# Grouped-query attention in two layers on one core: every scaling of the probabilities on GpSimd as a product of two tensors, and VectorE's copy of turned probabilities ahead of a row maximum

## The chip, the core and the metric

The kernel runs on one core of a Trainium2 chip. The core has engines that each work through their own list of instructions in order: TensorE (PE, with its weight loads PEld), VectorE (DVE), ScalarE (ACT), GpSimd (POOL) and SyncE (SP, which here only starts transfers). They meet at semaphores alone: an instruction that waits holds up everything behind it on its engine. The metric is the device time of one execution in microseconds (us), as a median of several executions. The clock of TensorE has two levels, 1.2 and 2.4 GHz; a profile shows the share that was granted (1.00 is 2.4 GHz).

## The reference, cut to what matters

The program is two transformer layers on 16 sequences of 512 tokens with 256 features. The change lies in the first layer's attention, which has 16 query heads and 4 key/value heads of width 64:

```
scores = einsum('bhqd,bhkd->bhqk', Q, K_rep) / scale
scores = scores + polarity_bias + (1.0 - gtp) * NEG
attn = softmax(scores, axis=-1)
out = einsum('bhqk,bhkd->bhqd', attn, V_rep)
```

The mask in it is causal, so a tile of 128 queries needs only the keys up to its own end. The layer goes on with a projection, a second attention with 16 heads of width 16, and a mixture of experts; the second layer has an attention and a feed-forward part of its own.

## The kernel before, in words

The first layer works on one sequence after another. The time of one sequence is a frame of 128 beats, numbered r = 0 to 127 in the code; each engine's list is written by a loop over the beats, and for each beat a chain of `if r ...` lines says which functions are called, in which order. That hand-written order is the only thing that decides what stands behind what. Beats 0 to 63 belong to the narrow attention, beats 64 to 127 to the grouped-query attention; small matrix products of other parts ("fills") are strewn between.

The grouped-query half takes 32 pairs p = 4g + qt: g = 0 to 7 is a pair of query heads, qt = 0 to 3 the tile of 128 queries, and i = 0 or 1 the head in the pair. I call the four pairs of one g a group, i = 0 the even and i = 1 the odd part. A part with qt has (qt + 1) * 128 key columns: 128, 256, 384 or 512. A part goes through these stations:

- TensorE, `scores_g` (L699): both parts of two neighbouring pairs (qt 0 and 1, or qt 2 and 3) at once, every fourth beat.
- VectorE, `biased_max` (L974): adds the bias, writes the sum to `prob` and takes the negative row maximum.
- ScalarE, `exponentials_g` (L1248): the exponential in place, and the row sums.
- VectorE, `reciprocal_g` (L980): the reciprocals of both sums of a pair.
- GpSimd, `scale` (L1420): multiplies the part by the reciprocal. In the odd parts of qt 0 and 1 VectorE does this, inside `reciprocal_g` (L984).
- TensorE, `turn_g` (L710): turns the 128x128 tiles into PSUM bank 4 (even) or 5 (odd); a part waits until that bank was copied out for the pair before.
- The copy of the turned part to SBUF: on VectorE for the even part (`copy_g`, L993), on ScalarE for the odd one (`copy_g`, L1258).
- TensorE, `values_g` (L727): the products with V, after every second pair.

The stations of a pair lie some beats apart. At the beats r = 64 + 2p and the next, TensorE issues the scores of pairs p and p + 1 (p even) and then turns pair p - 3; VectorE takes the maxima of pair p, the reciprocal of pair p - 1 and the copy of pair p - 3. ScalarE's list is written so:

```
if r >= 65:
    exponentials_g(f, (r - 65) // 2, (r - 65) % 2)
if r >= 72 and r % 2 == 0:
    copy_g(f, (r - 72) // 2)
```

so that it does the even and the odd exponential of pair p, and behind the odd one the copy of the odd part of pair p - 3. No fill of TensorE stands between the turning of qt = 3 and that of the next qt = 0 in four of the seven groups of a frame that reach it; where qt 1 and 2 are turned, there nearly always is one.

Of the kernel before, what the change touches and what calls it, by code (L numbers as in the profile page):

```python
# [23 lines left out]
P = 128  # L24
# [425 lines left out]
def layer0(nc, a, x1_d, xf_d, gt_d, bias_d, K):  # L450

    ctx = ExitStack()
    with ctx:
# [81 lines left out]
        def bias_of(h):  # L535
# [8 lines left out]
            sem(n) for n in ("scores_ready", "max_ready", "split", "max_turned", "max_placed", "t_ready", "exp_ready", "pv_ready", "out_turned"))  # L544
        s.g_scores, s.g_max, s.g_exp, s.g_recip, s.g_scaled, s.g_scaled_v, s.g_turned, s.g_copied_v, s.g_copied_a, s.g_pv, s.g_out = (
            sem("g_" + n) for n in ("scores", "max", "exp", "recip", "scaled", "scaled_v", "turned", "copied_v", "copied_a", "pv", "out"))
        s.w_ready = sem("w_ready")
# [14 lines left out]
        def at(u):  # L562
            return u // UNITS, u % UNITS // (NT * H), u // H % NT, u % H

        def scaled_on_pool(p, i):
            return i == 0 or p % NT > 1

        def scaled(b, p, i):
            qt = p % NT
            if scaled_on_pool(p, i):  # L570
                return s.g_scaled, 6 * (PAIRS * b + p // NT) + (1, 2, 3, 5)[qt] + i
            return s.g_scaled_v, 2 * (PAIRS * b + p // NT) + qt + 1

# [63 lines left out]
        with nc.Block() as block:  # L637
            @block.tensor
            def _(pe):
# [62 lines left out]
                def turn_g(b, p, i):  # L702
                    qt = p % NT
                    v = UNITS * b + 2 * p + i
                    if p == 0:
                        pe.wait_ge(s.exp_ready, UNITS * (b + 1))
                    pe.wait_ge(*scaled(b, p, i))
                    wait(pe, (s.g_copied_v, s.g_copied_a)[i], BEATS * b + p)
# [229 lines left out]
            def _(dve):  # L938
# [38 lines left out]
                def reciprocal_g(b, p):  # L977
                    k = 2 * p
                    dve.wait_ge(s.g_exp, UNITS * b + 2 * p + 2)
                    nc.vector.reciprocal(recip_g[:, k:k + 2], sums_g[:, k:k + 2]).then_inc(s.g_recip, 1)  # L980
                    if not scaled_on_pool(p, 1):
                        dve.wait_ge(s.g_recip, BEATS * b + p + 1)
                        v = prob[p % NT][:, 1, :]
                        nc.vector.tensor_scalar(v, v, recip_g[:, k + 1:k + 2], None, ALU.mult).then_inc(s.g_scaled_v, 1)  # L984

# [144 lines left out]
                for n in range(FIRST, LAST):  # L1130
                    f, r = n // FRAME, n % FRAME
                    c = f + 1
                    if there(f):
                        if r < 64:
                            row_max(UNITS * f + r)
                        if r >= 64:
                            biased_max(f, (r - 64) // 2, r % 2)
                        if r >= 67 and r % 2:
                            reciprocal_g(f, (r - 67) // 2)
                        if r >= 71 and r % 2:  # L1140
                            copy_g(f, (r - 71) // 2)
                    if there(f - 1):
                        if r == 1:
                            reciprocal_g(f - 1, 31)
                        if r in (1, 3, 5):
                            copy_g(f - 1, 29 + (r - 1) // 2)
                        if r == 28:
# [251 lines left out]
            def _(pool):  # L1399
# [16 lines left out]
                def scale(b, p, i):  # L1416
                    qt = p % NT
                    k = 2 * p + i
                    pool.wait_ge(s.g_recip, BEATS * b + p + 1)
                    nc.gpsimd.tensor_scalar(prob[qt][:, i, :], prob[qt][:, i, :], recip_g[:, k:k + 1], None, ALU.mult).then_inc(s.g_scaled, 1)  # L1420

# [39 lines left out]
                for n in range(FIRST, LAST):  # L1461
# [6 lines left out]
                    if there(f):  # L1468
                        if r < 64 and r % 4 == 3:
                            split(QUADS * f + r // 4)  # L1470
                        if r >= 68:
                            if scaled_on_pool((r - 68) // 2, r % 2):
                                scale(f, (r - 68) // 2, r % 2)
                        if r in (6, 8, 12, 13, 17, 18):
# [906 lines left out]
```

## Time and profile before

| | |
|---|---|
| median of 3 runs | 4328.75 us (4321.15 to 4343.08) |
| the profiled execution | 4331.27 us |
| its span, first to last instruction | 4329.4 us |
| mean granted clock | 0.974 |
| busy: TensorE / VectorE / ScalarE / GpSimd | 90% / 69% / 60% / 56% of the span |

The span has the first layer's sixteen frames (to about 2780 us; the copies of `Wo`, one at each frame's end, are started at 259.57, 429.71, 600.98 us and so on, some 168 us apart), then the experts and the second layer. A row of the timeline gives start, duration, engine, line, operation, tiles, and in brackets how long the engine had been idle before it and for whom. Starts and durations are those of one execution; durations of matmuls are partly modelled, so a step that ends on TensorE is best read from start to start.

### The profile page before, as it was taken

To read this page: it belongs to the slowest core of one execution; us is meant where nothing else is said; L and a number is where in the kernel's file an instruction comes from. 1 tells how busy PE (TensorE), PEld (TensorE's weight loads), DVE (VectorE), ACT (ScalarE), POOL (GpSimd) and SP (SyncE) were. 2 spreads that over 40 slices of the span, in tenths; PEclk is the share of its full clock that TensorE was granted. 3 is DMA by queue.
4 is the path that set the end of the run, shared out by engine and by line. 5 is a ranking of instruction groups with operands and counts; after the bars stand their busy time and mean duration, and the time that the engine had idled before them with its cause. 6 is when DMAs were issued, how large, how long until landed. Compare 5 with 4: busy or idle time off the path is not lost. (4 is left out here: it accounts for less than half of the span.)

```text
span 4329.4 us, 105712 instructions
## 1 busy us (share of the span) xinstructions
PE 3895.7 (90%) x37596; PEld 2560.4 (59%) x37596; DVE 3007.5 (69%) x8821; ACT 2581.9 (60%) x6209; POOL 2412.5 (56%) x3854
## 2 busy tenths in 40 slices
PE   3999999999999999999999999739599999999998
PEld 1565656556656556656565566526366666666666
DVE  4676776776777767767767676561577778778786
ACT  2656556556566566565565565402377777777776
POOL 3656557566576575565665664525455545555552
PEclk7999999999999999999999999959799999999999
DMA  4323334334243243343342432223422424334231
GB/s 128 72 77 86 80 76 94 74 89 94 59 104 79 70 91 77 75 89 79 84 94 66 97 83 66 69 75 61 66 53 48 69 46 59 61 48 68 46 56 26
DMA packets 168566, 317.06 MB, mean 73 GB/s; under 512 B 21680, under 2 KB 112112, under 8 KB 162928
## 3 DMA queue, kind: packets, MB, share of 16 engines
q1 hardware_dynamic: 162928, 300.88, 32.6%
q0 software_dynamic: 3968, 5.25, 0.7%
q8 instruction: 305, 5.00, 0.5%
q10 hardware_dynamic: 1152, 4.19, 0.3%
q14 instruction: 213, 1.74, 0.2%
HBM read 126.66 MB, written 32.59 MB: 37 GB/s over the span
## 5 line engine op out<-in xcount | busy, mean ns | idle before, releaser
L1420 POOL TENSOR_SCALAR l_prob_wo<-l_prob_wo,l_recip_g 128x384 f32<-128x384 f32 (+3 forms) x768 | 926.8, 1217 | 265.5 <-DVE l_recip_g L980 261.5
L1871 DVE TENSOR_REDUCE l_neg_max<-l_bank 128x1 f32<-128x512 f32 x1024 | 680.2, 684 | 260.6 <-PE l_bank L1710 258.9
L1997 ACT ACTIVATE l_pts<-l_bank 128x512 f32<-128x512 f32 x1024 | 593.0, 596 | 297.3 <-PE l_bank L1725 288.4
L1248 ACT ACTIVATE l_prob_wo<-l_prob_wo,l_neg_max_g 128x128 f32<-128x128 f32 (+3 forms) x1024 | 571.2, 559 | 299.1 <-DVE l_neg_max_g L974 293.2
L961 DVE CUSTOM_DVE_ANT_0 l_bank<-l_bank,l_mask 128x128 f32<-128x128 f32 (+3 forms) x1024 | 500.7, 500 | 318.0 <-PE l_bank L648 309.7
L1240 ACT ACTIVATE l_pts<-l_bank 128x128 f32<-128x128 f32 (+3 forms) x1024 | 437.3, 436 | 424.3 <-PE l_bank L666 407.7
L974 DVE CUSTOM_DVE_ANT_0 l_prob_wo<-l_bank,l_bias 128x128 f32<-128x128 f32 (+3 forms) x1024 | 475.9, 483 | 285.8 <-PE l_bank L699 263.3
L710 PE MATMUL l_bank<-ident,l_prob_wo 128*128 128x128 f32 x2560 | 428.4, 284 | 83.6 <-POOL l_prob_wo L1420 40.5
L710 PEld LDWEIGHTS l_bank<-ident,l_prob_wo 128*128 128x128 f32 x2560 | 291.0, 141 | 318.0 <-issue 180.1
L1710 PE MATMUL l_bank<-next_ks,l_qs 96*128 96x512 bf16 x1024 | 393.5, 385 | 46.6 <-DVE l_neg_max L1871 23.2
L1725 PEld LDWEIGHTS l_bank<-l_qs,next_ks 128*128 128x128 bf16 x4096 | 303.5, 97 | 181.3 <-ACT l_pts L1997 30.6
L1725 PE MATMUL l_bank<-l_qs,next_ks 128*128 128x128 bf16 x4096 | 395.4, 218 | 0.9 <-ACT l_pts L1997 0.7
L699 PE MATMUL l_bank<-l_kT,l_qT 64*128 64x128 f32 (+3 forms) x2048 | 356.3, 462 | 24.7 <-DVE l_neg_max_g L974 22.0
L2085 POOL CAST next_max_parts<-l_neg_max 128x4 bf16<-128x4 f32 x256 | 71.3, 278 | 514.5 <-DVE l_neg_max L1871 514.5
L648 PE MATMUL l_bank<-l_ks,l_qs 96*128 96x128 bf16 (+3 forms) x1024 | 307.3, 305 | 55.5 <-DVE l_neg_max L961 43.8
L741 PE MATMUL l_bank<-l_xnT,l_w 128*128 128x512 f32 x640 | 340.8, 616 | 0.3 <-DVE l_arena L1016 0.3
L727 PE MATMUL l_bank<-l_pts,l_v 128*64 128x256 f32 (+1 forms) x3072 | 334.7, 353 | 2.6 <-ACT l_pts L1258 0.8
L665 PE MATMUL l_bank<-l_qs,l_ks 128*128 128x128 bf16 x2560 | 310.0, 220 | 21.9 <-ACT l_pts L1240 20.7
L1408 POOL CAST l_max_parts<-l_neg_max 128x4 bf16<-128x4 f32 x256 | 49.4, 193 | 502.0 <-DVE l_neg_max L961 501.7
L665 PEld LDWEIGHTS l_bank<-l_qs,l_ks 128*128 128x128 bf16 x2560 | 197.5, 98 | 157.9 <-ACT l_pts L1240 61.8
L764 PE MATMUL l_bank<-l_prob_wo,l_outT 128*128 128x256 f32 x1024 | 274.5, 393 | 12.4 <-DVE l_bias L1016 9.2
L1739 PE MATMUL l_bank<-l_pts,next_vpad 128*32 128x128 f32 x8192 | 277.0, 275 | 4.6 <-ACT l_pts L1997 1.0
(262 smaller groups left out, 8042.7 us busy)
## 6 DMA issues: line engine op xcount, KB each, us to landing
l_bias<-bias SPq DMA_DIRECT2D x128, 512.0 KB, 4.4
l_qs<-l_parts SPq DMA_DIRECT2D x192, 128.0 KB
l_qs<-l_qs SPq DMA_DIRECT2D x96, 256.0 KB
l_x<-in_x SPq DMA_DIRECT2D x32, 512.0 KB, 5.0
l_kT<-l_bias SPq DMA_DIRECT2D x128, 128.0 KB, 3.2
l_qT<-l_arena SPq DMA_DIRECT2D x128, 128.0 KB, 3.0
l_qT<-l_bias SPq DMA_DIRECT2D x128, 128.0 KB, 3.0
l_prob_wo<-in_Wo SPq DMA_DIRECT2D x16, 1024.0 KB, 4.7
```

What stands on the lines that cost most here:

```text
L665: m = nc.tensor.matmul(to[:, j * P:(j + 1) * P], ks[:, h, j * P:(j + 1) * P], qs[:, h, qt * P:(qt + 1) * P], start=True, stop=j < qt)
L699: nc.tensor.matmul(G4[(v + i) % 4][:, 0:w], qT[half, g, qt * P:(qt + 1) * P], kT[half, g // 2, 0:w], start=True, stop=True).then_inc(s.g_s ...
L710: m = nc.tensor.transpose(PT[i][:, j * P:(j + 1) * P], prob[qt][:, i, j * P:(j + 1) * P], ident[:, :])
L961: nc.vector.tensor_tensor_reduce(S[u % 2][:, 0:w], S[u % 2][:, 0:w], mask[:, T - w:T], -1.0, 3.0e38, ALU.add, ALU.min, neg_max[:, k:k + 1] ...
L974: nc.vector.tensor_tensor_reduce(prob[qt][:, i, :], G4[v % 4][:, 0:w], bias[:, g % 2, i, T - w:T], -1.0 / ROOT, 3.0e38, ALU.add, ALU.min, ...
L1240: nc.scalar.activation(pts[:, q % 2, i, 0:w, :], TB[u % 2][:, 0:w * P].rearrange("p (j q) -> p j q", j=w), ACT.Exp, scale=DS ** -0.5).then ...
L1248: nc.scalar.activation(prob[qt][:, i, :], prob[qt][:, i, :], ACT.Exp, bias=neg_max_g[:, k:k + 1], scale=-1.0, accum_out=sums_g[:, k:k + 1] ...
L1420: nc.gpsimd.tensor_scalar(prob[qt][:, i, :], prob[qt][:, i, :], recip_g[:, k:k + 1], None, ALU.mult).then_inc(s.g_scaled, 1)
L1710: nc.tensor.matmul(S[n % SB][:, :], qs[b % 2][0:96, h, qt * P:(qt + 1) * P], ks[b % 2][0:96, h, :], start=True, stop=True).then_inc(s.scor ...
L1725: m = nc.tensor.matmul(TB[u % 2][:, j * P:(j + 1) * P], ks[b % 2][:, h, j * P:(j + 1) * P], qs[b % 2][:, h, qt * P:(qt + 1) * P], start=Tr ...
L1871: nc.vector.tensor_reduce(neg_max[:, n % (2 * UNITS):n % (2 * UNITS) + 1], S[n % SB][:, :], AX.X, ALU.max, negate=True).then_inc(s.max_rea ...
L1997: nc.scalar.activation(pts[:, q % 2, u % H, :, :], TB[u % 2][:, :].rearrange("p (j q) -> p j q", j=NT), ACT.Exp, scale=DS ** -0.5).then_in ...
```

## The change

All scalings go to GpSimd, in the order of the parts, and one semaphore counts them. The instruction is another: a product of two tensors, the second being one column of reciprocals repeated along the row, where it was a product of a tensor with a scalar per row. VectorE loses its scaling of the odd parts of qt 0 and 1, and its `copy_g` moves: it stands between the even and the odd row maximum of a beat pair, where it stood behind the odd maximum and the reciprocal.

```
-                    pe.wait_ge(*scaled(b, p, i))
+                    pe.wait_ge(s.g_scaled, UNITS * b + 2 * p + i + 1)
...
                     nc.vector.reciprocal(recip_g[:, k:k + 2], sums_g[:, k:k + 2]).then_inc(s.g_recip, 1)
-                    if not scaled_on_pool(p, 1):
-                        dve.wait_ge(s.g_recip, BEATS * b + p + 1)
-                        v = prob[p % NT][:, 1, :]
-                        nc.vector.tensor_scalar(v, v, recip_g[:, k + 1:k + 2], None, ALU.mult).then_inc(s.g_scaled_v, 1)
...
                         if r < 64:
                             row_max(UNITS * f + r)
+                        if r >= 71 and r % 2:
+                            copy_g(f, (r - 71) // 2)
                         if r >= 64:
                             biased_max(f, (r - 64) // 2, r % 2)
                         if r >= 67 and r % 2:
                             reciprocal_g(f, (r - 67) // 2)
-                        if r >= 71 and r % 2:
-                            copy_g(f, (r - 71) // 2)
                     if there(f - 1):
+                        if r in (1, 3, 5):
+                            copy_g(f - 1, 29 + (r - 1) // 2)
                         if r == 1:
                             reciprocal_g(f - 1, 31)
-                        if r in (1, 3, 5):
-                            copy_g(f - 1, 29 + (r - 1) // 2)
...
                     pool.wait_ge(s.g_recip, BEATS * b + p + 1)
-                    nc.gpsimd.tensor_scalar(prob[qt][:, i, :], prob[qt][:, i, :], recip_g[:, k:k + 1], None, ALU.mult).then_inc(s.g_scaled, 1)
+                    v = prob[qt][:, i, :]
+                    nc.gpsimd.tensor_tensor(v, v, recip_g[:, k:k + 1].to_broadcast([P, (qt + 1) * P]), ALU.mult).then_inc(s.g_scaled, 1)
...
                         if r >= 68:
-                            if scaled_on_pool((r - 68) // 2, r % 2):
-                                scale(f, (r - 68) // 2, r % 2)
+                            scale(f, (r - 68) // 2, r % 2)
```

VectorE's list before, at a place in the first frame where the maxima of a pair with qt = 2 are taken (the rows with 128x384; the row behind each is the reading of the accumulator) and the even part of qt = 3 of the group before is copied (128x4x128); the semaphores that a row waits for stand in brackets:

```order
L974 ISA l_prob_wo,l_neg_max_g<-l_bank,l_bias 128x384 [waits l0_g_turned,l0_g_scores]
L974 ISA l_neg_max_g 128x1
L974 ISA l_prob_wo,l_neg_max_g<-l_bank,l_bias 128x384 [waits l0_g_turned,l0_g_scores]
L974 ISA l_neg_max_g 128x1
L980 RECIPROCAL l_recip_g<-l_sums_g 128x2 [waits l0_g_exp]
L984 TENSOR_SCALAR l_prob_wo<-l_prob_wo,l_recip_g 128x256 [waits l0_g_recip]
L993 COPY l_pts<-l_bank 128x4x128 [waits l0_g_pv,l0_g_turned]
L974 ISA l_prob_wo,l_neg_max_g<-l_bank,l_bias 128x512 [waits l0_g_turned,l0_g_scores]
```

The same place of VectorE's list in the changed kernel, where the lines have other numbers (L965 is the maximum, L971 the reciprocal, L980 the copy):

```order
L965 ISA l_prob_wo,l_neg_max_g<-l_bank,l_bias 128x384 [waits l0_g_turned,l0_g_scores]
L965 ISA l_neg_max_g 128x1
L980 COPY l_pts<-l_bank 128x4x128 [waits l0_g_pv,l0_g_turned]
L965 ISA l_prob_wo,l_neg_max_g<-l_bank,l_bias 128x384 [waits l0_g_turned,l0_g_scores]
L965 ISA l_neg_max_g 128x1
L971 RECIPROCAL l_recip_g<-l_sums_g 128x2 [waits l0_g_exp]
L965 ISA l_prob_wo,l_neg_max_g<-l_bank,l_bias 128x512 [waits l0_g_turned,l0_g_scores]
```

The copy, with its wait for the turning, now stands ahead of the odd maximum and of the reciprocal, and the scaling L984 is gone.

GpSimd's list before, for two groups of the first frame:

```order
L1420 TENSOR_SCALAR l_prob_wo<-l_prob_wo,l_recip_g 128x128 [waits l0_g_recip]
L1420 TENSOR_SCALAR l_prob_wo<-l_prob_wo,l_recip_g 128x256 [waits l0_g_recip]
L1420 TENSOR_SCALAR l_prob_wo<-l_prob_wo,l_recip_g 128x384 [waits l0_g_recip] x2
L1420 TENSOR_SCALAR l_prob_wo<-l_prob_wo,l_recip_g 128x512 [waits l0_g_recip] x2
L1420 TENSOR_SCALAR l_prob_wo<-l_prob_wo,l_recip_g 128x128 [waits l0_g_recip]
```

And in the changed kernel (L1408 is the scaling there):

```order
L1408 TENSOR_TENSOR l_prob_wo<-l_prob_wo,l_recip_g 128x128 [waits l0_g_recip] x2
L1408 TENSOR_TENSOR l_prob_wo<-l_prob_wo,l_recip_g 128x256 [waits l0_g_recip] x2
L1408 TENSOR_TENSOR l_prob_wo<-l_prob_wo,l_recip_g 128x384 [waits l0_g_recip] x2
L1408 TENSOR_TENSOR l_prob_wo<-l_prob_wo,l_recip_g 128x512 [waits l0_g_recip] x2
L1408 TENSOR_TENSOR l_prob_wo<-l_prob_wo,l_recip_g 128x128 [waits l0_g_recip] x2
```

A group has eight scalings where it had six; nothing else moves on GpSimd. The lists of ScalarE and TensorE keep their order.

## Rows read from the trace of the kernel before

**Rows 1.** Windows: length, busy (instructions) of PE, PEld, DVE, ACT, POOL; clock, DMA, GB/s.
```profile
1179.00:1275.00 96.00, 88.51 (x667) 56.43 (x666) 66.41 (x249) 65.97 (x204) 73.11 (x65) 1.00 0.40 83
```

**Rows 2.** Waits of PE from 150 to 2800 us: total, times, longest.
```profile
PE l_bank L710 <- POOL l_prob_wo L1420: 40.5, 67, 1.5
PE l_bank L710 <- DVE l_pts L993: 26.0, 47, 1.2
...
PE l_bank L710 <- ACT l_pts L1258: 15.8, 45, 0.5
```

**Rows 3.** The page's part 5: the scalings on GpSimd (busy us, mean ns).
```profile
L1420 POOL TENSOR_SCALAR l_prob_wo<-l_prob_wo,l_recip_g 128x384 f32<-128x384 f32 (+3 forms) x768 | 926.8, 1217 | 265.5 <-DVE l_recip_g L980 261.5
```

**Rows 4.** Groups by form, POOL: products and sums of two tensors.
```profile
L1426 POOL TENSOR_TENSOR l_bias<-l_bias 128x512 f32<-128x512 f32 x96 | 120.5, 1269 | 98.3 <-DVE l_bias L1016 98.3
...
L1447 POOL TENSOR_TENSOR l_dense<-l_blocks,l_recip 128x256 f32<-128x256 f32 x64 | 39.7, 620 | 0.0
...
L2122 POOL TENSOR_TENSOR l_prevT<-l_prevT 128x512 f32<-128x512 f32 x32 | 33.2, 1040 | 0.8
```

**Rows 5.** Groups, DVE: the scalings on VectorE.
```profile
L984 DVE TENSOR_SCALAR l_prob_wo<-l_prob_wo,l_recip_g 128x128 f32<-128x128 f32 (+1 forms) x256 | 119.3, 466 | 9.2
```

**Rows 6.** Timeline, one half group: maxima of qt = 2, turning of qt = 3.
```profile
1227.87 0.56 DVE L974 CUSTOM_DVE_ANT_0 l_prob_wo<-l_bank,l_bias 128x384 f32<-128x384 f32 x1 [1.60 <-PE l_bank L699]
...
1228.35 0.55 DVE L974 CUSTOM_DVE_ANT_0 l_prob_wo<-l_bank,l_bias 128x384 f32<-128x384 f32 x1
1228.47 0.62 ACT L1248 ACTIVATE l_prob_wo<-l_prob_wo,l_neg_max_g 128x384 f32<-128x384 f32 x1 [1.76 <-DVE l_neg_max_g L974]
1228.63 1.09 PE L710 MATMUL l_bank<-ident,l_prob_wo 128*128 128x128 f32 x8
...
1229.08 0.60 ACT L1248 ACTIVATE l_prob_wo<-l_prob_wo,l_neg_max_g 128x384 f32<-128x384 f32 x1
...
1229.32 0.69 DVE L993 COPY l_pts<-l_bank 128x512 f32<-128x512 f32 x1
...
1229.76 0.58 ACT L1258 COPY l_pts<-l_bank 128x512 f32<-128x512 f32 x1
1229.93 0.68 DVE L974 CUSTOM_DVE_ANT_0 l_prob_wo<-l_bank,l_bias 128x512 f32<-128x512 f32 x1
```

**Rows 7.** Timeline, the half group one group earlier: turning of qt = 3 and 0.
```profile
1217.64 0.66 PE L710 MATMUL l_bank<-ident,l_prob_wo 128*128 128x128 f32 x4
...
1218.97 0.91 PE L710 MATMUL l_bank<-ident,l_prob_wo 128*128 128x128 f32 x5 [0.68 <-POOL l_prob_wo L1420]
...
1219.67 0.58 ACT L1258 COPY l_pts<-l_bank 128x512 f32<-128x512 f32 x1 [0.88 <-PE l_bank L710]
...
1220.40 0.30 PE L710 MATMUL l_bank<-ident,l_prob_wo 128*128 128x128 f32 x1 [0.51 <-ACT l_pts L1258]
```

**Rows 8.** Timeline: the same two instructions, first and last of seven in the frame.
```profile
1195.83 1.09 PE L710 MATMUL l_bank<-ident,l_prob_wo 128*128 128x128 f32 x8
...
1197.41 0.56 ACT L1258 COPY l_pts<-l_bank 128x512 f32<-128x512 f32 x1
...
1263.54 1.09 PE L710 MATMUL l_bank<-ident,l_prob_wo 128*128 128x128 f32 x8
...
1264.92 0.56 ACT L1258 COPY l_pts<-l_bank 128x512 f32<-128x512 f32 x1
```

**Rows 9.** Timeline, PE: two more of its waits in that frame.
```profile
1250.53 1.13 PE L699 MATMUL l_bank<-l_kT,l_qT 64*128 64x512 f32 x4 [1.42 <-DVE l_neg_max_g L974]
...
1259.96 0.55 PE L710 MATMUL l_bank<-ident,l_prob_wo 128*128 128x128 f32 x3 [1.10 <-POOL l_prob_wo L1420]
```

**Rows 10.** Timeline, PE: that wait in the second frame.
```profile
403.94 1.58 PE L699 MATMUL l_bank<-l_kT,l_qT 64*128 64x512 f32 x4 [1.67 <-DVE l_neg_max_g L974]
```

**Rows 11.** Windows around it (columns as in rows 1).
```profile
402.00:406.00 4.00, 2.33 (x9) 0.85 (x8) 2.84 (x11) 1.39 (x4) 1.17 (x2) 0.81 0.34 121
406.00:410.00 4.00, 4.00 (x29) 3.76 (x29) 3.38 (x13) 3.20 (x10) 1.96 (x2) 0.76 0.00 0
```

More of the change, by code:

```diff
@@ L544, in layer0 @@
             sem(n) for n in ("scores_ready", "max_ready", "split", "max_turned", "max_placed", "t_ready", "exp_ready", "pv_ready", "out_turned"))
-        s.g_scores, s.g_max, s.g_exp, s.g_recip, s.g_scaled, s.g_scaled_v, s.g_turned, s.g_copied_v, s.g_copied_a, s.g_pv, s.g_out = (
-            sem("g_" + n) for n in ("scores", "max", "exp", "recip", "scaled", "scaled_v", "turned", "copied_v", "copied_a", "pv", "out"))
+        s.g_scores, s.g_max, s.g_exp, s.g_recip, s.g_scaled, s.g_turned, s.g_copied_v, s.g_copied_a, s.g_pv, s.g_out = (
+            sem("g_" + n) for n in ("scores", "max", "exp", "recip", "scaled", "turned", "copied_v", "copied_a", "pv", "out"))
         s.w_ready = sem("w_ready")
@@ L563, in at @@
             return u // UNITS, u % UNITS // (NT * H), u // H % NT, u % H
[L565 to L572, printed above, removed]
         def there(c):
```

## The prediction

> **What bounds the kernel now.** I read the windows of a grouped-query half first. Of 96 us TensorE is busy 88.5, GpSimd 73, VectorE and ScalarE 66 each, at the full clock [rows 1]. So TensorE sets the pace, and another engine costs time only where TensorE waits for it. Then the waits of TensorE over the whole first layer: before the turnings (L710) it stood idle 40.5 us for the scalings, 26.0 us for VectorE's copies and 15.8 us for ScalarE's [rows 2]. These are what the change can win: per frame, a sixteenth, 2.5, 1.6 and 1.0 us. What it can lose is read from the timeline, where the stations of one half group stand one under the other [rows 6, 7]: there the reader is to see what an instruction waits for and what stands behind it on its own engine.
>
> **The scalings on GpSimd.** Before, 768 scalings take 926.8 us [rows 3], over 128 groups 7.24 us a group, of about 11 (the turning of qt = 3 starts at 1217.64 and at 1228.63 [rows 6, 7]). After, a group has eight products over 2 x 1280 columns. No row shows this instruction. The nearest, products by a repeated column and of a tensor with itself, take 620 ns for 256 and 1040 for 512 columns, that is 0.20 us and 1.64 ns a column; a sum of two full tensors takes 1269 ns for 512 [rows 4]. By the first a group costs 8 x 0.20 + 2560 x 0.00164 = 5.8 us, by the second in proportion 2560 x 2.48 ns = 6.3, and if a column cost as much as in the scalings of before (7.24 us over 2176 columns, 3.33 ns) 8.5. I take 5.8, since L1447 also has a repeated operand. With 8.5 it would still be below the 11 us of a group, though not by much where other work of GpSimd falls in the same group.
>
> Shorter scalings win where TensorE waits for them and for nothing later. A wait like the 0.68 us before the odd turning of qt = 3 [rows 7] lies in the stretch that the part on the copy replaces, so it is counted there. The 1.10 us before the odd turning of qt = 2 [rows 9], is mine to count: its scaling is 384 wide, by the line above 0.83 us instead of 1.2, so about 0.4 us a frame is won. Bounds: none (if products are no faster) to all of 40.5 / 16 = 2.5 us a frame.
>
> **The scalings taken from VectorE** are 256 instructions and 119.3 us [rows 5]. VectorE is idle for a third of this half and has just been waiting for scores when this stretch begins ([1.60 <-PE L699], rows 6), so this is worth nothing by itself. What it brings is that a copy behind it starts sooner, and that is counted with the copy. On GpSimd the odd part of qt = 0 and 1 comes one short product later, but its turning is due several us after the reciprocal: nothing.
>
> **The copy ahead of the odd maximum.** This decides, and it is worked out at the half group where the maxima of qt = 2 are taken and qt = 3 is turned. Call S the start of that turning on TensorE (1228.63). TensorE issues the scores first and turns afterwards. So VectorE has its even maximum done before S: the odd one starts at 1228.35, 0.28 us ahead of S, and the copy at 1229.32, S + 0.69 [rows 6]. Now the turning of four tiles needs 0.70 us until its copy can start (1218.97 to 1219.67 [rows 7]). The copy before already started the moment it could. Moved ahead, it can't start sooner there; it makes VectorE stand still from about 1228.4 until S + 0.70, with the odd maximum behind it.
>
> Behind the odd maximum hangs ScalarE, in order: the odd exponential, then the copy of the odd part of qt = 3. And TensorE turns the odd part of the next qt = 0 into the bank that this copy frees, with the products with V behind it, which need that copy too. The new chain from S, each step from start to start: turning to copy 0.70 [rows 7]; copy to odd maximum 0.61 (1229.32 to 1229.93); maximum to exponential 0.60 (1227.87 to 1228.47); exponential to ScalarE's copy 0.68 (1229.08 to 1229.76) [rows 6]; that copy to TensorE 0.73 (1219.67 to 1220.40 [rows 7]). ScalarE's copy starts at S + 2.59, TensorE goes on at S + 3.32.
>
> Before, ScalarE's copy started at S + 1.58 and + 1.38 in the first and the last of the seven such half groups of a frame [rows 8], at S + 2.03 [rows 7] and + 1.13 [rows 6] in two between: 1.53 in the mean. That already contains the waits for GpSimd, for both copies and the fills. The delay of TensorE is 2.59 - 1.53 = 1.06 us each, 7.4 us a frame. From the resumption to the next S TensorE goes through its own work, nearly without waits, so nothing gives this back.
>
> In the other half of a group (maxima of qt = 0, turning of qt = 1) the same chain exists, but copy, maximum and exponential are 128 to 256 wide, and a fill stands between the turnings; I take 0, and 0 to 0.3 us a frame as bounds. At the odd beats with maxima of qt = 1 and 3 the scores are there already and the products with V stand between: 0. The reciprocal comes later too, by the same 1.5 us, and the scalings behind it; these are due in the next half group, over 5 us later: 0.
>
> Once a frame TensorE waits 1.42 us for an odd maximum that is held up by the loading of x [rows 9]. After, a copy of 384 columns, some 0.5 us, stands ahead of that maximum; on the other side VectorE passes the point that releases the load about as much earlier, seen from TensorE. I take 0; bounds -1.4 to +0.5 us a frame.
>
> **The sum.** 7.4 - 0.4 = 7.0 us a frame, 16 frames: 112 us. The profiled execution took 4331.3 us, so 4443. Then the clock. In the new chain TensorE turns the even part of qt = 0 at about S + 1.43 (0.70 + 0.73), is done by S + 1.73, and stands idle 1.6 us until S + 3.32 wherever no fill comes between: 4 of 7, 64 times in all. An idle time of 1.67 us was followed by a granted clock of 0.81 and 0.76 over two stretches of 4 us [rows 10, 11], a loss of 4 x 0.19 + 4 x 0.24 = 1.7 us; the half with the 1.42 us kept 1.00 [rows 1, 9]. At 1.6 I let one in four fall: 16 x 1.7 = 27 us. Together 4470; the profiled execution lies 2.5 us above the median of 4328.75, so **4470 us** stands for the median too, 3.3% slower.
>
> **Rivals.**
>
> The clock falls at most of these gaps: 64 x 1.7 = 109 us instead of 27, 4552 us. For it: a shorter gap of 0.3 us lies just ahead of the 1.6. Against it: gaps of 1.42 did nothing. The Trainium skill ("TensorE: Matmul & The Clock Gate", section "HAM oscillation — how this bites in real kernels") says that a wait that recurs in a loop throttles the clock anew in each round, so that the price is paid as often as the wait comes. The trace agrees at the 1.67 us gap and shows no fall at 1.42.
>
> The relief comes and the chain does not: 40.5 + 26.0 us of waits go [rows 2], 4265 us. That needs VectorE to come to the copy later than S + 0.70, with other work ahead of it, so that the copy never waits and costs the odd maximum its own 0.61 us alone; from that point on the new order costs little and the relief decides. Against it: in rows 6 VectorE is there 0.28 us before S, one whole us too early.
>
> The chain is there but half of it is absorbed, because fills or later waits take up what TensorE loses: 56 us, 4387. For it: three of seven groups have a fill. Against it: both turnings of qt = 3 are done at S + 1.09 [rows 6], so a fill has 2.2 us to cover, and four of seven have none.
>
> No net change, relief and delay cancel: 4330. It needs 7 us of relief a frame where all three waits together are 5.1.
>
> **How the numbers follow.** Forecast (the chain, few falls of the clock) 0.60; clock at most gaps 0.18; half absorbed 0.09; relief 0.08; no net change 0.05. The first three are slower: 0.87. The runs of before spread by 0.5%, so 0.5% is what can be told from no change: within it 0.05, faster 0.08. The range goes from just below the half-absorbed case, 4380, to above the case with the clock, 4590, which takes in the open bounds of x and of the fills; relief, no change and a little above are left out. The forecast's own range is 4430 to 4510.
>
> **What would show it.** Right: in rows 6's place the copy on VectorE comes ahead of the odd maximum and is preceded by idle time for L710's turning; TensorE's idle time before L710 for ScalarE's copy grows from 15.8 us to well above 100, in the longest single case from 0.5 to over 1.5 us; waits for scalings fall to a few us; GpSimd's busy time falls by about 180 us (1.4 x 128) and VectorE's by about 119; the frames are some 177 us apart instead of 168. Second layer and experts keep their length. Wrong: if ScalarE's copy still starts about 1.5 us after S, or TensorE's waits for it stay at 1 us a frame, the chain is not what I think; if the clock falls below 0.97 in the grouped halves, the second case has come; if the products take over 1.5 us for 512 columns, GpSimd is late again.

## The result, and the profile after

The changed kernel takes 4478.64 us (median, 4473.48 to 4491.71) against 4331.32 us before: ratio 1.0338, 95% interval 1.0320 to 1.0356. It is slower by 147 us; 4470 was forecast. The frames start some 177 us apart, as forecast (`Wo` at 800.00, 977.19, 1155.12, 1332.35 us). Below, the kernel before is "before" and the changed one "after"; the span after is 4476.1 us at a mean granted clock of 0.961 (before 4329.4 and 0.974).

Three parts of the page of the kernel after: busy time by engine, and the groups of the scalings (L1408), turnings (L701) and VectorE's copies (L980), as in [rows 3].

```profile
PE 3953.6 (88%) x37596; PEld 2592.8 (58%) x37596; DVE 2914.5 (65%) x8565; ACT 2585.4 (58%) x6209; POOL 2202.4 (49%) x4110
...
L1408 POOL TENSOR_TENSOR l_prob_wo<-l_prob_wo,l_recip_g 128x128 f32<-128x128 f32 (+3 forms) x1024 | 722.4, 726 | 593.2 <-DVE l_recip_g L971 591.9
...
L701 PE MATMUL l_bank<-ident,l_prob_wo 128*128 128x128 f32 x2560 | 440.1, 285 | 172.9 <-POOL l_prob_wo L1408 86.1
...
L980 DVE COPY l_pts<-l_bank 128x128 f32<-128x128 f32 (+3 forms) x512 | 249.1, 486 | 244.0 <-PE l_bank L701 183.5
```

GpSimd has 210 us less to do and VectorE 93 us less, and the program is slower all the same. The last row tells where to look: VectorE now stands idle 183.5 us ahead of its copies, waiting for turnings, where it was 23.8 us in the kernel before:

```profile
L993 DVE COPY l_pts<-l_bank 128x128 f32<-128x128 f32 (+3 forms) x512 | 246.5, 481 | 42.3 <-PE l_bank L710 23.8 <-PE l_bank L680 17.8
```

The row of L701 seems to say that TensorE waits most for GpSimd's scalings. That reading is wrong, as experiment 3 shows.

The timeline of one half group of the kernel after, the place of [rows 6, 7]: maxima of qt = 2 (128x384), turning of qt = 3 (x8), then the even and the odd part of the next qt = 0 (x1 each).

```profile
1279.58 0.56 DVE L965 CUSTOM_DVE_ANT_0 l_prob_wo<-l_bank,l_bias 128x384 f32<-128x384 f32 x1 [1.86 <-PE l_bank L690]
...
1280.33 1.09 PE L701 MATMUL l_bank<-ident,l_prob_wo 128*128 128x128 f32 x8
...
1281.03 0.69 DVE L980 COPY l_pts<-l_bank 128x512 f32<-128x512 f32 x1 [0.89 <-PE l_bank L701]
1281.64 0.55 DVE L965 CUSTOM_DVE_ANT_0 l_prob_wo<-l_bank,l_bias 128x384 f32<-128x384 f32 x1
...
1281.87 0.30 PE L701 MATMUL l_bank<-ident,l_prob_wo 128*128 128x128 f32 x1 [0.44 <-DVE l_pts L980]
...
1282.23 0.61 ACT L1235 ACTIVATE l_prob_wo<-l_prob_wo,l_neg_max_g 128x384 f32<-128x384 f32 x1 [1.34 <-DVE l_neg_max_g L965]
1282.35 1.18 POOL L1408 TENSOR_TENSOR l_prob_wo<-l_prob_wo,l_recip_g 128x256 f32<-128x256 f32 x2 [3.48 <-DVE l_recip_g L971]
...
1282.84 0.56 ACT L1245 COPY l_pts<-l_bank 128x512 f32<-128x512 f32 x1
...
1283.55 0.30 PE L701 MATMUL l_bank<-ident,l_prob_wo 128*128 128x128 f32 x1 [1.38 <-POOL l_prob_wo L1408]
```

With S = 1280.33: copy at S + 0.70, odd maximum + 1.31, odd exponential + 1.90, ScalarE's copy + 2.51, TensorE + 3.22. In the other six half groups of this frame ScalarE's copy comes at S + 2.50 or + 2.51 too. Once the copy waits for its turning, every step behind it is bound to S, and the spread of before (S + 1.13 to + 2.03, [rows 6 to 8]) is gone. Over all 112 such half groups of the trace the copy lies at S + 2.52 in the mean, before at S + 1.52.

The last row blames GpSimd. The odd part of qt = 0 was scaled in the products of 128 columns long before; what GpSimd ended at 1283.53, just ahead of that start, are the 256 wide products of qt = 1 (L1408 at 1282.35, two of them), which this turning doesn't read. ScalarE's copy at 1282.84 plus the 0.71 us from a copy to TensorE is 1283.55, the start itself.

The waits of TensorE from 150 to 2900 us in the kernel after (total, times, longest), beside [rows 2]:

```profile
PE l_bank L701 <- POOL l_prob_wo L1408: 84.4, 87, 1.4
PE l_bank L701 <- ACT l_pts L1245: 60.3, 49, 1.4
...
PE l_bank L690 <- DVE l_neg_max_g L965: 23.1, 14, 2.8
PE l_bank L701 <- DVE l_pts L980: 22.7, 52, 0.4
```

A window of the grouped half of that frame, and two stretches of 4 us at its end and behind it (columns as in [rows 1, 11]):

```profile
1229.00:1325.00 96.00, 82.95 (x610) 52.84 (x612) 55.86 (x215) 61.74 (x189) 56.92 (x75) 0.97 0.38 83
```

```profile
1321.00:1325.00 4.00, 2.62 (x14) 1.48 (x15) 2.60 (x11) 2.86 (x8) 2.59 (x4) 0.72 0.00 0
1325.00:1329.00 4.00, 4.00 (x25) 2.23 (x22) 1.56 (x8) 1.76 (x6) 1.33 (x2) 0.85 0.01 2
```

TensorE is busy 83.0 of 96 us where it was 88.5 [rows 1]. Behind the gap that ended at 1322.50 the clock shows 0.72 and 0.85; behind the equal gap that ended at 1283.55 it did not fall.

### The profile page after: what moved, and what is told of

Same layout as the page of the kernel before. It is cut to its first block and busy times, and to the rows that moved or that the text cites. A ratio compares the mean times of both kernels' runs of the same rounds, so it can differ in the third digit from the quotient of the medians.

```text
span 4476.1 us, 105712 instructions
## 1 busy us (share of the span) xinstructions
PE 3953.6 (88%) x37596; PEld 2592.8 (58%) x37596; DVE 2914.5 (65%) x8565; ACT 2585.4 (58%) x6209; POOL 2202.4 (49%) x4110
## 5 line engine op out<-in xcount | busy, mean ns | idle before, releaser
L1408 POOL TENSOR_TENSOR l_prob_wo<-l_prob_wo,l_recip_g 128x128 f32<-128x128 f32 (+3 forms) x1024 | 722.4, 726 | 593.2 <-DVE l_recip_g L971 591.9
L965 DVE CUSTOM_DVE_ANT_0 l_prob_wo<-l_bank,l_bias 128x128 f32<-128x128 f32 (+3 forms) x1024 | 489.2, 480 | 382.9 <-PE l_bank L690 382.1
L701 PE MATMUL l_bank<-ident,l_prob_wo 128*128 128x128 f32 x2560 | 440.1, 285 | 172.9 <-POOL l_prob_wo L1408 86.1
L701 PEld LDWEIGHTS l_bank<-ident,l_prob_wo 128*128 128x128 f32 x2560 | 297.8, 143 | 409.3 <-POOL l_prob_wo L1408 209.9
L980 DVE COPY l_pts<-l_bank 128x128 f32<-128x128 f32 (+3 forms) x512 | 249.1, 486 | 244.0 <-PE l_bank L701 183.5
L690 PE MATMUL l_bank<-l_kT,l_qT 64*128 64x128 f32 (+3 forms) x2048 | 366.1, 473 | 25.8 <-DVE l_neg_max_g L965 23.1
L718 PE MATMUL l_bank<-l_pts,l_v 128*64 128x256 f32 (+1 forms) x3072 | 376.5, 386 | 0.8 <-ACT l_pts L1245 0.8
L718 PEld LDWEIGHTS l_bank<-l_pts,l_v 128*64 128x64 f32 x3072 | 217.9, 148 | 131.5 <-issue 56.3
```

The source lines that it names most:

```text
L701: m = nc.tensor.transpose(PT[i][:, j * P:(j + 1) * P], prob[qt][:, i, j * P:(j + 1) * P], ident[:, :])
L718: m = nc.tensor.matmul(OT[64 * i:64 * (i + 1), 2 * P * k + skip:2 * P * (k + 1)], v0[:, j, g // 2, :], pts_g[:, k, i, j, skip:2 * P], star ...
L965: nc.vector.tensor_tensor_reduce(prob[qt][:, i, :], G4[v % 4][:, 0:w], bias[:, g % 2, i, T - w:T], -1.0 / ROOT, 3.0e38, ALU.add, ALU.min, ...
L1408: nc.gpsimd.tensor_tensor(v, v, recip_g[:, k:k + 1].to_broadcast([P, (qt + 1) * P]), ALU.mult).then_inc(s.g_scaled, 1)
```

## The experiments

All ratios are to the kernel before, run beside each kernel on the same chip.

**1. The copy order alone.** The kernel before with only VectorE's copy moved (the diff of the frame's end goes with it).

```
+                        if r >= 71 and r % 2:
+                            copy_g(f, (r - 71) // 2)
                         if r >= 64:
                             biased_max(f, (r - 64) // 2, r % 2)
                         if r >= 67 and r % 2:
                             reciprocal_g(f, (r - 67) // 2)
-                        if r >= 71 and r % 2:
-                            copy_g(f, (r - 71) // 2)
```

> The kernel before, with the copy of VectorE alone moved ahead of the odd maximum (and of the reciprocal); all scalings as before. Theory of the chain (turning of qt = 3, VectorE's copy, odd maximum, odd exponential, ScalarE's copy, TensorE): the whole loss is here, without the small relief of the shorter scalings, so some 7 to 9 us a frame, 4440 to 4500 us; ScalarE's copy of qt = 3 starts at S + 2.5 in the seven half groups of a frame. Theory that the scalings are what TensorE now waits for (the waits of L701 in the changed kernel are put down to GpSimd for 86.1 us, to ScalarE for 60.8): the products aren't in this kernel, its time lies near 4331 us. Theory of the clock: it falls wherever the gap of 1.6 us stands, so slow too; the share of the clock shows in the granted clock of the grouped halves.

4529.24 us, ratio 1.0463 (1.0445 to 1.0480): slower still than the whole change, and 29 us above the upper end that I gave. ScalarE's copy of qt = 3 starts at S + 2.57 in the mean of the 112 half groups, as the chain has it. The whole loss is in this edit, and it is 201 us, not 147; the rest of the change must win some 50. With the old scalings the waits carry the other name:

```profile
PE l_bank L710 <- ACT l_pts L1258: 100.9, 87, 1.4
PE l_bank L710 <- POOL l_prob_wo L1420: 53.1, 74, 1.5
```

**2. The scalings alone.** The kernel after with VectorE's copy back behind the odd maximum and the reciprocal (the frame's end goes back with it, here and in experiments 4, 6, 7, 9 and 11).

```
-                        if r >= 71 and r % 2:
-                            copy_g(f, (r - 71) // 2)
                         if r >= 64:
                             biased_max(f, (r - 64) // 2, r % 2)
                         if r >= 67 and r % 2:
                             reciprocal_g(f, (r - 67) // 2)
+                        if r >= 71 and r % 2:
+                            copy_g(f, (r - 71) // 2)
```

> The changed kernel with VectorE's copy back behind the odd maximum and the reciprocal; all scalings stay on GpSimd as products of two tensors. Theory of the chain: nothing of the loss is left, and the relief from shorter scalings shows alone: 0.4 to 2.5 us a frame, 4290 to 4325 us, ScalarE's copy of qt = 3 again some 1.5 us after S. Theory that the scalings on GpSimd are what TensorE waits for: the loss stays, above 4400 us.

4289.46 us, ratio 0.9914 (0.9897 to 0.9930), half a us below the range by the chain. The chain's numbers hold, and this version beats both kernels. In its timeline the odd maximum precedes the copy again, and ScalarE's copy is at S + 1.14 (S = 1198.64):

```profile
1198.37 0.55 DVE L965 CUSTOM_DVE_ANT_0 l_prob_wo<-l_bank,l_bias 128x384 f32<-128x384 f32 x1
...
1198.64 1.09 PE L701 MATMUL l_bank<-ident,l_prob_wo 128*128 128x128 f32 x8
...
1199.34 0.69 DVE L980 COPY l_pts<-l_bank 128x512 f32<-128x512 f32 x1 [0.33 <-PE l_bank L701]
...
1199.78 0.59 ACT L1245 COPY l_pts<-l_bank 128x512 f32<-128x512 f32 x1
...
1200.18 0.63 PE L701 MATMUL l_bank<-ident,l_prob_wo 128*128 128x128 f32 x2 [0.44 <-DVE l_pts L980]
```

VectorE's copy starts 0.70 us after S in both orders (0.74 here and 0.71 in the kernel after, as means of the 112 half groups). Moving it ahead of the maximum did not make it one step earlier; it only made the maximum later.

This kernel also splits the loss. The busy row of its page:

```profile
PE 3883.7 (91%) x37596; PEld 2559.2 (60%) x37596; DVE 2922.5 (68%) x8565; ACT 2583.9 (60%) x6209; POOL 2206.6 (51%) x4110
```

| | span | TensorE busy | the rest |
|---|---|---|---|
| before | 4329.4 | 3895.7 | 433.7 |
| scalings alone | 4285.8 | 3883.7 | 402.1 |
| after | 4476.1 | 3953.6 | 522.5 |

The scalings win 43.6 us (12.0 busy, 31.6 idle). The copy then costs 190.3: 120.4 us of idle time, and 69.9 us in which TensorE takes longer over the same 37596 matmuls.

**3. ScalarE's copy ahead of its exponentials**, in the kernel after; reciprocals, scalings and VectorE's order stay.

```
-                        if r >= 65:
-                            exponentials_g(f, (r - 65) // 2, (r - 65) % 2)
                         if r >= 72 and r % 2 == 0:
                             copy_g(f, (r - 72) // 2)
+                        if r >= 65:
+                            exponentials_g(f, (r - 65) // 2, (r - 65) % 2)
```

> The changed kernel with one edit on ScalarE: the copy of the odd part stands ahead of the exponentials of a beat, so that it no longer waits for the odd maximum that VectorE's copy holds up. Theory of the chain: ScalarE's copy starts when the odd turning is done, S + 1.1 to 1.6, TensorE goes on at S + 2.3 at most, and most of the 147 us is won back: 4310 to 4390 us, although VectorE's copy and the odd maximum stay as late as in the changed kernel. Theory that late reciprocals and scalings (GpSimd) hold TensorE: the odd exponential is later still, so the time stays at 4480 us or above.

4352.46 us, ratio 1.0059 (1.0043 to 1.0076): one swap on ScalarE takes back 126 of the 147 us. The link between odd exponential and ScalarE's copy was the one that carried the delay to TensorE. And the label is settled: nothing about GpSimd was touched, yet the waits put down to it fall from 84.4 to 11.0 us.

```profile
PE l_bank L690 <- DVE l_neg_max_g L965: 42.8, 46, 2.6
...
PE l_bank L701 <- POOL l_prob_wo L1408: 11.0, 16, 0.9
...
PE l_bank L701 <- ACT l_pts L1245: 6.5, 17, 0.5
```

What remains above experiment 2 is 57 us of span. The first row has 25 of them: the odd maximum is still held up by the copy, and scores wait for it 42.8 us instead of 17.9. Another 31 are busy time of TensorE, 3914.9 us instead of 3883.7; the trace's record of the clock shows why. In the fifteen frames between the first and the last copy of `Wo` it falls seven times to the lower level, for 58 us together (29 us lost); in experiment 2 it never falls there. Each of the seven falls comes at the frame's longest wait of scores, 2.35 to 2.63 us, for the maximum that the load of x holds up, as here:

```profile
1252.08 1.65 PE L690 MATMUL l_bank<-l_kT,l_qT 64*128 64x512 f32 x4 [2.63 <-DVE l_neg_max_g L965]
```

**4. The copy between odd maximum and reciprocal**, in the kernel after.

```
-                        if r >= 71 and r % 2:
-                            copy_g(f, (r - 71) // 2)
                         if r >= 64:
                             biased_max(f, (r - 64) // 2, r % 2)
+                        if r >= 71 and r % 2:
+                            copy_g(f, (r - 71) // 2)
                         if r >= 67 and r % 2:
                             reciprocal_g(f, (r - 67) // 2)
```

> The changed kernel with VectorE's copy between the odd maximum and the reciprocal: the maximum is as early as before, only the reciprocal and the scalings behind it are as late as in the changed kernel. Theory of the chain: the reciprocal has over 5 us to spare, so as fast as with the copy behind both, 4290 to 4330 us. Theory that late reciprocals make GpSimd's scalings late: most of the loss is here, above 4400 us.

4294.93 us, ratio 0.9929 (0.9911 to 0.9947). A reciprocal behind the copy costs at most a few us. It is the maximum that must not stand there.

**5. The gap filled with useless work**, in the kernel after, to see the clock's share.

```
-                    for j in range(qt + 1):
+                    for j in [0] * (8 if p and p % NT == 0 and i == 0 else 0) + list(range(qt + 1)):
                         m = nc.tensor.transpose(PT[i][:, j * P:(j + 1) * P], prob[qt][:, i, j * P:(j + 1) * P], ident[:, :])
```

> The changed kernel with work of no use for TensorE: where the even part of qt = 0 is turned, behind a qt = 3, its one tile is turned nine times instead of once, some 0.9 us that lie in the gap of 1.4 us before the odd turning. The chain keeps its length. Against the kernel with the copy behind the maximum, the changed one has 120 us more of TensorE's idle time and 70 us more of its busy time for the same instructions. If the 70 us are a clock that falls because of these gaps, the clock of the grouped half rises to 0.99 or 1.00 and the time falls by 40 to 70 us, to 4410 to 4440 us. If the clock falls for another reason, or its falls cost less than I count, the time stays at 4479 us or grows by up to 15 us, since one group of seven has a gap of only 0.3 us.

4431.49 us, ratio 1.0239 (1.0213 to 1.0266): 896 turnings more, and 47 us less than the kernel after. In a half group with S = 1263.77 TensorE still goes on at S + 3.21, so the chain is as long as it was, but the idle 1.38 us are now 0.51:

```profile
1263.77 1.09 PE L701 MATMUL l_bank<-ident,l_prob_wo 128*128 128x128 f32 x8
1265.30 1.17 PE L701 MATMUL l_bank<-ident,l_prob_wo 128*128 128x128 f32 x9 [0.44 <-DVE l_pts L980]
1266.98 0.30 PE L701 MATMUL l_bank<-ident,l_prob_wo 128*128 128x128 f32 x1 [0.51 <-POOL l_prob_wo L1408]
```

Windows over the first layer (columns as in [rows 1]), of the kernel after, of this one, and of the scalings alone:

```profile
200.00:2700.00 2500.00, 2260.43 (x18444) 1442.64 (x18439) 1577.85 (x5798) 1443.26 (x3966) 1279.97 (x2229) 0.97 0.32 78
```

```profile
200.00:2700.00 2500.00, 2333.84 (x19548) 1530.08 (x19546) 1605.61 (x5901) 1472.21 (x4064) 1306.34 (x2264) 1.00 0.33 80
```

```profile
200.00:2700.00 2500.00, 2355.47 (x19798) 1516.28 (x19796) 1695.60 (x6216) 1545.47 (x4258) 1363.48 (x2383) 1.00 0.35 83
```

The granted clock goes from 0.97 to 1.00, the upper level of 2.4 GHz nearly throughout. TensorE's busy time is 3988.9 us; eight repeats take 1.17 - 0.30 = 0.87 us, all 896 some 97, so the instructions of before take some 3891.5, 62 us less than in the kernel after. These 62 of the 70 us were clock, lost because of the gaps: in the fifteen frames the clock falls 36 times in the kernel after, for 130 us together (65 us lost), and twice in this one, while the waits at the load of x stay (waits of scores for maxima 23.1 and 22.6 us). In the kernel after 23 of the 36 falls come within 1.4 us of the end of a gap of 1.38 us; the other 13 come at the wait for the load of x or up to 7 us behind it, and nearly all of these go too when the gaps are filled.

**6 and 7. Which of the four copies.** In the kernel after the copy stands ahead for qt = 3 alone, and then for the other three alone.

```
-                        if r >= 71 and r % 2:
+                        if r >= 71 and r % 2 and (r - 71) // 2 % NT == 3:
                             copy_g(f, (r - 71) // 2)
                         if r >= 64:
                             biased_max(f, (r - 64) // 2, r % 2)
                         if r >= 67 and r % 2:
                             reciprocal_g(f, (r - 67) // 2)
+                        if r >= 71 and r % 2 and (r - 71) // 2 % NT != 3:
+                            copy_g(f, (r - 71) // 2)
```

(for the second kernel == and != change places)

> The changed kernel with VectorE's copy ahead of the odd maximum for qt = 3 alone; for qt = 0, 1 and 2 it stands behind the maximum and the reciprocal again. Theory of the chain: the seven half groups of a frame are all of the loss, 4460 to 4485 us. Rival, that the copies of qt = 1 (same place of the beat, shorter tiles) or of qt = 0 and 2 share in it: 4300 to 4440 us.

> The changed kernel with VectorE's copy ahead of the odd maximum for qt = 0, 1 and 2, and behind maximum and reciprocal for qt = 3. With qt = 3 alone ahead it was 4464 us, with all ahead 4479, with all behind 4289. Theory of the chain: the copies of qt = 0, 1 and 2 cost next to nothing, 4285 to 4310 us, and ScalarE's copy of qt = 3 is back at S + 1.1 to 1.7. If any copy ahead of a maximum opens the chain, it is above 4400 us.

qt = 3 alone: 4464.00 us, ratio 1.0315 (1.0288 to 1.0343), 175 us above experiment 2. The others alone: 4318.27 us, ratio 0.9967 (0.9950 to 0.9985), 29 us above it and 8 above my range. In the spans these are 174.3 us (110.2 of idle time of TensorE, 64.1 busy) and 24.0 us (7.0 idle, 17.0 busy). The seven half groups that I worked out are most of the loss. My "0" for the other copies was low. Their idle time is nearly all one wait: scores wait 24.1 us for maxima instead of 17.9. In one frame of that kernel the wait for the odd maximum held up by the load of x is 2.00 us, where it was 0.94 in experiment 2, and the scores behind it are slow, 1.52 us instead of 1.13.

```profile
1247.82 1.52 PE L690 MATMUL l_bank<-l_kT,l_qT 64*128 64x512 f32 x4 [2.00 <-DVE l_neg_max_g L965]
```

```profile
1230.08 1.13 PE L690 MATMUL l_bank<-l_kT,l_qT 64*128 64x512 f32 x4 [0.94 <-DVE l_neg_max_g L965]
```

**8 to 10. What the scalings bring, taken apart.** First the kernel before with products on GpSimd, VectorE keeping its 256 scalings; then all 1024 scalings on GpSimd by the old instruction, copy behind; then the first of these with VectorE's copy ahead of reciprocal and scaling.

```
-                    nc.gpsimd.tensor_scalar(prob[qt][:, i, :], prob[qt][:, i, :], recip_g[:, k:k + 1], None, ALU.mult).then_inc(s.g_scaled, 1)
+                    v = prob[qt][:, i, :]
+                    nc.gpsimd.tensor_tensor(v, v, recip_g[:, k:k + 1].to_broadcast([P, (qt + 1) * P]), ALU.mult).then_inc(s.g_scaled, 1)
```

> The kernel before with one edit: GpSimd's 768 scalings are products of two tensors; VectorE keeps its 256, and the copy stays behind the maximum. All scalings on GpSimd as products, with the copy behind, gave 4289 us against 4328. If the shorter scalings alone bring that, this kernel is at 4285 to 4300 us; if taking 256 scalings from VectorE brings a good part, it is at 4305 to 4325 us. My prediction had 0.4 us a frame for the first and nothing for the second.

> All 1024 scalings on GpSimd as before's product with a scalar per row, none on VectorE, VectorE's copy behind maximum and reciprocal. The products alone, with VectorE's 256 scalings kept, gave 4339 us, no gain; with both edits it is 4289. If taking the scalings from VectorE is the gain by itself, this kernel is at 4285 to 4305 us. If the two belong together (GpSimd's old scalings, now 8.5 us a group, are late without the shorter instruction), it is at 4320 us or above, with TensorE's waits for scalings at 40 us or more.

> The kernel with the products alone (VectorE keeps its 256 scalings, 4339 us) with one more edit: VectorE's copy stands ahead of the reciprocal and VectorE's scaling, behind the odd maximum. There VectorE's scaling of 256 columns took 0.80 us beside a product on GpSimd, where it had taken 0.35 beside the old scaling, and the copy behind it started at S + 1.13 in place of S + 0.69. If this longer scaling ahead of the copy is what ate the gain of the shorter scalings, the scaling stays at 0.80 us here, the copy starts at S + 0.69, and the time is 4285 to 4305 us. If the products bring nothing for another reason, it stays at 4325 to 4345 us.

Products alone: 4339.22 us, 1.0022 (1.0010 to 1.0035). The move alone: 4344.39 us, 1.0025 (1.0011 to 1.0039). Products with the copy ahead of the scaling: 4333.55 us, 0.9999 (0.9987 to 1.0010). None of the three wins anything; experiment 2, with both edits, wins 0.9%.

The move alone fails as one of its two cases said: the old instruction takes 1099.4 us for 1024, 8.6 us a group, and TensorE's waits put down to GpSimd are 50.7 us.

The products alone fail for something that I did not foresee. VectorE's scaling and GpSimd's product start on the same reciprocal and run side by side. In the kernel with products alone, and then in the kernel before:

```profile
1219.24 1.09 PE L710 MATMUL l_bank<-ident,l_prob_wo 128*128 128x128 f32 x8
...
1219.64 0.80 DVE L984 TENSOR_SCALAR l_prob_wo<-l_prob_wo,l_recip_g 128x256 f32<-128x256 f32 x1
1219.68 0.61 POOL L1421 TENSOR_TENSOR l_prob_wo<-l_prob_wo,l_recip_g 128x256 f32<-128x256 f32 x1 [0.64 <-DVE l_recip_g L980]
...
1220.37 0.68 DVE L993 COPY l_pts<-l_bank 128x512 f32<-128x512 f32 x1
```

```profile
1207.46 1.09 PE L710 MATMUL l_bank<-ident,l_prob_wo 128*128 128x128 f32 x8
...
1207.86 0.35 DVE L984 TENSOR_SCALAR l_prob_wo<-l_prob_wo,l_recip_g 128x256 f32<-128x256 f32 x1
1207.91 1.08 POOL L1420 TENSOR_SCALAR l_prob_wo<-l_prob_wo,l_recip_g 128x256 f32<-128x256 f32 x1 [1.27 <-DVE l_recip_g L980]
...
1208.15 0.69 DVE L993 COPY l_pts<-l_bank 128x512 f32<-128x512 f32 x1
```

The same instruction of VectorE takes 0.80 us beside the product, until just behind the product's end at 1220.29, and 0.35 beside the old scaling; in the kernel with products alone all 128 scalings of this width take 0.80 us. The copy behind it starts at S + 1.13 instead of S + 0.69, and TensorE's waits for VectorE's copies grow from 26.0 us [rows 2] to 75.2, while those for scalings fall from 40.5 to 8.2: one wait took the other's place.

My cure, the copy ahead of that scaling, did not bring the gain: the copy starts at S + 0.70 again and the waits for it are 30.0 us, but what now stands behind the 0.80 us is the next maximum. In the half group with S = 1205.71 the odd maximum of qt = 3 starts at S + 4.03, in the same half group of experiment 2 (S = 1188.54) at S + 3.20; the means of the 112 half groups are S + 3.60 and + 2.69. The scores wait for it, in experiment 2 they do not:

```profile
1209.74 0.68 DVE L974 CUSTOM_DVE_ANT_0 l_prob_wo<-l_bank,l_bias 128x512 f32<-128x512 f32 x1
...
1210.48 0.70 PE L699 MATMUL l_bank<-l_kT,l_qT 64*128 64x256 f32 x4 [0.51 <-DVE l_neg_max_g L974]
```

```profile
1191.74 0.68 DVE L965 CUSTOM_DVE_ANT_0 l_prob_wo<-l_bank,l_bias 128x512 f32<-128x512 f32 x1
...
1192.31 0.93 PE L690 MATMUL l_bank<-l_kT,l_qT 64*128 64x128 f32 x8
```

So VectorE's scaling beside the products costs on whichever side of the copy it stands. How much is shown only in part: of the 45 us of span above experiment 2, 12 are these waits for maxima (29.8 us instead of 17.9), 9 other idle time and 24 busy time of TensorE, of which falls of the clock explain some 7 (14 us at the lower level in the fifteen frames). Whether the 0.35 us that it takes undisturbed would have cost as well was not tried.

**11. ScalarE's copy first, in the kernel of experiment 2** (the edit of experiment 3).

> The kernel with all scalings on GpSimd as products and VectorE's copy behind the odd maximum, and ScalarE's copy of the odd part ahead of the exponentials of its beat. TensorE there still waits 10.8 us for ScalarE's copies; if these are late because an exponential stands ahead of them, 4275 to 4285 us. If the copy then waits for its turning, with the odd exponential behind it, the maxima and scores come later, and it is at 4290 to 4340 us.

4287.99 us, ratio 0.9903 (0.9879 to 0.9927): between my two cases, and not to be told from experiment 2. The waits of the scores for maxima rise from 17.9 to 22.1 us. The two kernels of experiments 2 and 11 are the fastest, 39 and 44 us below the kernel before.

## Why the prediction was right, and where it was not

**The chain: right, step by step.** 0.70, 0.61, 0.60, 0.68 and 0.73 us were forecast, 0.70, 0.61, 0.59, 0.61 and 0.71 came; TensorE goes on at S + 3.22 instead of 3.32. The term was 1.06 us in seven half groups of sixteen frames, 118 us; TensorE's idle time grew by 120.4 (experiment 2 to after). Taken apart, the copy of qt = 3 alone adds 110.2 us of idle time and the other copies 7.0 (experiments 6 and 7), so hardly any luck is in it; the four half groups from which I took S + 1.53 stand for all 112, whose mean is S + 1.52.

**The clock: right in kind, too small.** I let one gap in four fall, 27 us; the runs show 70, of which filling the gaps gave back 62. The clock fell 36 times in fifteen frames (experiment 5), where I had 16 in sixteen and the rival at most gaps 64; in the kernel before it falls 4 times. The gaps were shorter than I had them, 1.38 us and not 1.6, and more: 1.15 us also stood in two of the three groups with a fill, 96 gaps instead of 64. So my argument that gaps of 1.42 us did nothing [rows 1, 9] was too weak: it rested on one gap, and 23 of 1.38 us were followed by a fall, one of them behind 1322.50. The grouped half shows 0.97, the bound below which I would have called the rival true.

**The scalings: the step that failed.** "Worth nothing by itself" for VectorE's 256 scalings, and 0.4 us a frame for the shorter products: 6 us in all. The products were sized well, 726 ns in the mean over the four widths, 5.8 us a group as forecast, and each edit alone does win nothing. But together they win 44 us of span. I priced the two one by one from the kernel before, with 466 ns for VectorE's scaling [rows 5], and did not ask what the new instruction does to the neighbour that the same change removes. The trace of before could have told. The 466 ns mix two widths, and the narrower takes longer:

```profile
L984 DVE TENSOR_SCALAR l_prob_wo<-l_prob_wo,l_recip_g 128x128 f32<-128x128 f32 x128 | 70.8, 553 | 4.6
...
L984 DVE TENSOR_SCALAR l_prob_wo<-l_prob_wo,l_recip_g 128x256 f32<-128x256 f32 x128 | 48.5, 379 | 4.6
```

One of 128 columns takes 0.29 us where only a scaling of the same width starts beside it on GpSimd, and up to 1.04 where GpSimd is at sums and differences of two tensors (L1431).

The Trainium skill has a rule that bears on this ("SBUF — State Buffer", section "Who interferes with whom"): VectorE, for a product with a scalar in its two-port mode, and GpSimd share a pair of SBUF ports, which the instruction that issues first holds until its end while the other stands still. The 0.80 us beside the product agree in that one of the two stands still, though it is VectorE, whose row starts 0.04 us before the product's. The 0.35 us beside GpSimd's old scaling, itself 1.08 us long, do not agree, and there the measurement decides: in this kernel not every instruction of GpSimd blocks VectorE.

**The sum.** 118 + 27 - 6 = 139 forecast; 120.4 + 69.9 - 43.6 = 146.7 in the spans. The clock's 43 us too little and the scalings' 38 us too little cancel. That is luck: the forecast of the time was better than its terms.

**The signs.** Right: the order on VectorE with idle time ahead of the copy, the frames' 177 us, the 0 for the load of x (waits of scores for maxima 22.0 us before, 23.1 after), the experts and second layer (1550 us behind the last copy of `Wo`, 1549 before), the busy times (GpSimd -210 us, more than the 180 I gave; VectorE -93, where 119 were its scalings). Wrong as written: the waits for ScalarE's copy were to pass 100 us and those for scalings to fall to a few, and the profile shows 60.3 and 84.4, the longest at 1.4 us where I had over 1.5. Their sum, 144.7 us, is 124 above the 21.1 of experiment 2 (10.8 and 10.3), which is the chain; the name beside it was the profile's guess.

**The rivals.** Relief without the chain did exist, at 4289 us, but only with the copy left where it was. That the chain is half absorbed is refuted by the 120.4 us of idle time that the copy adds, where this rival had 56 for it. The clock at most gaps came halfway: 70 us instead of the 109 of this rival.

## What to carry to other kernels

An instruction that waits belongs behind what is ready: moved ahead, it starts no sooner if its input sets its start, and all that stands behind it is bound to that input. Price two edits of one change together where both touch engines that run side by side, since each can be worth nothing alone. And where the engine named as a releaser ended work that the waiting instruction doesn't read, go back along the buffers: the wait is another's.

## What was not expected of the hardware

- VectorE's scaling of 256 columns takes 0.35 us beside GpSimd's product with a scalar per row (113 of 128 cases in the kernel before), and 0.80 beside GpSimd's product of two tensors (all 128 in experiment 8), which itself takes 0.61.
- On GpSimd the product with a repeated column takes 412, 628, 828 and 1045 ns for 128 to 512 columns, and the product with a scalar per row 639, 1043, 1243 and 1568: the form with two tensors is the faster.

In experiment 2 by form (busy us, mean ns), and in the kernel before:

```profile
L1408 POOL TENSOR_TENSOR l_prob_wo<-l_prob_wo,l_recip_g 128x512 f32<-128x512 f32 x256 | 263.9, 1045 | 11.0 <-DVE l_recip_g L971 10.6
...
L1408 POOL TENSOR_TENSOR l_prob_wo<-l_prob_wo,l_recip_g 128x128 f32<-128x128 f32 x256 | 100.1, 412 | 71.5 <-DVE l_recip_g L971 71.5
```

```profile
L1420 POOL TENSOR_SCALAR l_prob_wo<-l_prob_wo,l_recip_g 128x512 f32<-128x512 f32 x256 | 399.5, 1568 | 2.5 <-DVE l_recip_g L980 2.1
...
L1420 POOL TENSOR_SCALAR l_prob_wo<-l_prob_wo,l_recip_g 128x128 f32<-128x128 f32 x128 | 81.8, 639 | 23.3 <-DVE l_recip_g L980 23.3
```
